# Splitting the next batch's queries inside attention, with a head's loads first on SyncE

## What is computed

```python
q = (x @ Wq.T + bq)...; k = (x @ Wk.T + bk)...; v = (x @ Wv.T + bv)...   # 16 heads of 16 dims
sim = jnp.einsum('bhid,bhjd->bhij', q, k) / sqrt(16) / (abs(temperature)[0] + 0.1)
for fi, freq in enumerate([31., 37., 41., 43., 47.]):
    scores = scores + alpha[:, fi] * jnp.sin(TWO_PI * sim / freq + phi[:, fi])
w = jax.nn.sigmoid(scores);  w = w / (jnp.sum(w, axis=-1, keepdims=True) + 1e-10)
out = jnp.einsum('bhij,bhjd->bhid', w, v)
```

## Time and profile before

| | us |
|---|---|
| median of 3 runs | 7117.2 (7109.4 to 7120.61) |
| the profiled execution's own time | 7120.0 |
| its span, first to last instruction | 7118.2 |
| projection, to attention's first DMA | 412.6 |
| TensorE, VectorE, ScalarE busy | 6113.5, 5773.2, 5853.0 |
| granted TensorE clock, mean | 0.934 |

### The profile page before, as it was taken

The page is one execution under the profiler, slowest core; times in us unless marked ns, Lnnn a source line. Parts: engine busy times, 40 slices in busy tenths (PEclk is TensorE's granted clock), DMA queues, the critical chain, the costliest instruction groups (busy, mean ns, idle before and its releaser), DMA issues. The chain is left out here.

```text
span 7118.2 us, 130314 instructions
## 1 busy us (share of the span) xinstructions
PE 6113.5 (86%) x48057; PEld 4363.9 (61%) x48057; DVE 5773.2 (81%) x4353; ACT 5853.0 (82%) x5874; POOL 205.8 (3%) x217
## 2 busy tenths in 40 slices
PE   6539999999999999999999999999999999826555
PEld 3326666666666666666666666666666666625444
DVE  6648888888888888888888888888888888857775
ACT  1139999999999999999999999999999999901111
POOL 0000000000000000000000000000000000010000
PEclk8769999999999999999999999999999999966666
DMA  7931111111111111111111111111111111131220
GB/s 291 358 143 47 47 47 46 46 47 46 45 47 45 45 47 47 47 46 47 46 47 46 47 47 46 47 45 46 47 45 46 47 45 47 30 81 46 50 52 20
DMA packets 322961, 446.10 MB, mean 63 GB/s; under 512 B 158980, under 2 KB 189604, under 8 KB 321384
## 3 DMA queue, kind: packets, MB, share of 16 engines
q1 hardware_dynamic: 317032, 432.81, 19.4%
q0 software_dynamic: 5376, 5.30, 0.3%
HBM read 284.11 MB, written 153.75 MB: 62 GB/s over the span
## 5 line engine op out<-in xcount | busy, mean ns | idle before, releaser
L593 ACT ACTIVATE a_wave<-a_ps_turn 128x1024 f32<-128x1024 f32 x5120 | 4915.0, 1365 | 132.2 <-PE a_ps_turn L527 131.9
L527 PE MATMUL a_ps_turn<-a_q_r,a_k_r 64*128 64x512 f32 x20480 | 3392.0, 399 | 399.8 <-ACT a_wave L593 249.3
L609 DVE SCALAR_TENSOR_TENSOR a_weight<-a_wave,a_head_c,a_weight 128x2048 f32<-128x2048 f32 x1536 | 3612.6, 2352 | 59.5
L527 PE MATMUL a_ps_turn<-a_q_r,a_rounder 64*128 64x512 f32 x20480 | 3241.4, 392 | 4.6 <-issue 4.6
L527 PEld LDWEIGHTS a_ps_turn<-a_q_r,a_k_r 64*128 64x128 f32 x20480 | 1951.8, 185 | 1574.9 <-ACT a_wave L593 804.5
L527 PEld LDWEIGHTS a_ps_turn<-a_q_r,a_rounder 64*128 64x128 f32 x20480 | 1976.6, 186 | 244.6 <-issue 9.4
L609 DVE SCALAR_TENSOR_TENSOR a_weight<-a_wave,a_head_c 128x2048 f32<-128x2048 f32 x512 | 1203.9, 2351 | 844.4 <-ACT a_wave L593 844.4
L587 ACT ACTIVATE a_weight<-a_weight,a_head_c 128x2048 f32<-128x2048 f32 x512 | 1186.0, 2316 | 5.2 <-DVE a_weight L609 5.2
L547 PE MATMUL a_ps_out<-a_weight,a_v_r 128*32 128x512 f32 x4096 | 547.2, 606 | 7.6 <-ACT a_weight L587 5.4
L506 POOL COPY a_head_c<-a_table 128x5 f32 (+1 forms) x128 | 114.3, 893 | 5596.2 <-ACT a_weight L587 5596.1
L547 PEld LDWEIGHTS a_ps_out<-a_weight,a_v_r 128*32 128x32 f32 x4096 | 80.8, 108 | 194.7 <-issue 184.0
(11 more groups left out here) (231 smaller groups left out, 1919.3 us busy)
## 6 DMA issues: line engine op xcount, KB each, us to landing
q_d<-p_q_hl SPq DMA_DIRECT2D x80, 1024.0 KB, 8.3
a_q_r<-q_d SPq DMA_DIRECT2D x256, 320.0 KB
a_k_r<-k_d SPq DMA_DIRECT2D x512, 128.0 KB
a_q_r<-q_d SPq DMA_DIRECT2D x256, 160.0 KB
k_d<-p_k_hl SPq DMA_DIRECT2D x8, 4096.0 KB, 15.2
a_k_r<-k_d SPq DMA_DIRECT2D x512, 64.0 KB
o_d<-a_out SPq DMA_DIRECT2D x512, 34.0 KB
num<-o_d SPq DMA_DIRECT2D x32, 512.0 KB
```

The lines of the kernel that those rows point to most:

```text
L527: last = nc.tensor.matmul(ps_turn[slot_of(r, s, f)][:, half, :], exact(w(rows[half])), exact(q_r[rows[half], k, f, :]), start=(i == 0), st ...
L593: nc.scalar.activation(wave[:, s // 2 % 2, f, s % 2, :], ps_turn[slot_of(r, s, f)][:].rearrange("p a b -> p (a b)"), ACT.Sin, scale=TURN_I ...
L609: return v.scalar_tensor_tensor(both(weight[:, i, :, :]), both(wave[:, i % 2, f, :, :]), head_c[:, k, f:f + 1], to, ALU.mult, ALU.add)
```

## The change

The projection stores the whole queries of each batch (`qk_sb` to a new `q_d` of 1 MB a batch), and splits only batch 0, whose split queries go to `qs_d`. The split of batch b+1 is made during attention over batch b: in heads 1 to 8 of the 16, two parts a head. A part is 128 features by 128 tokens (`QW`), fetched from `q_d`, scaled for all five frequencies in one TENSOR_TENSOR, rounded in a CAST, subtracted in another TENSOR_TENSOR, and stored in two DMAs. The buffers are double. The loops of SyncE and VectorE now run over batches with 16 heads written out. On SyncE the loads for the next head come first, then the stores of one part, the result's store, the stores of the second part, and the fetches of the next two parts.

```diff
@@ project_qkv, SyncE
-                def keep(b):
+                def keep(b, split=False):
+                    sp.wait_ge(q_ready, b + 1)
+                    sp.dma_start(q_d[b, :, :].rearrange("(m p) l -> p m l", p=P), qk_sb[:, 0, :, :]).then_inc(whole_kept, 16)
                     sp.wait_ge(v_ready, b + 2)
                     sp.dma_start(v_d[b, :, :, :], v_sb[:]).then_inc(v_kept, 16)
-                    for m in range(KC):
-                        for f in range(NF):
-                            sp.wait_ge(q_split, NF * (KC * b + m) + f + 1)
-                            sp.dma_start(q_d[b, :, m * P:(m + 1) * P, f, :].rearrange("i p l -> p i l"),
-                                         q_hl[:, f, :, :]).then_inc(q_kept[f], 16)
+                    if split:
+                        for m in range(KC):
+                            for f in range(NF):
+                                sp.wait_ge(q_split, NF * m + f + 1)
+                                sp.dma_start(qs_d[b, :, m * P:(m + 1) * P, f, :].rearrange("i p l -> p i l"),
+                                             q_hl[:, f, :, :]).then_inc(q_kept[f], 16)
...
@@ project_qkv, VectorE
-                with dve.Fori(0, B, 1) as b:
+                def body(b, split):
+
                     dve.wait_ge(q_summed, b + 1)
+                    dve.wait_ge(whole_kept, 16 * (b + 1))
...
-                    split_q(b, 0)
+                    if split:
+                        dve.wait_ge(q_ready, b + 1)
+                        dve.wait_ge(rate_in, 32)
+                        split_q(0)
...
-                    split_q(b, 1)
                     dve.wait_ge(k_ready, b + 2)
                     dve.wait_ge(k_kept, 16 * (b + 1))
...
+                    if split:
+                        split_q(1)
+                        dve.wait_ge(q_split, NF * KC)
+                body(0, True)
+                with dve.Fori(1, B, 1) as b:
+                    body(b, False)
@@ oscillatory_attention, SyncE
+                for m in range(KC):
+                    sp.dma_start(rate[:, m, :], tab_d[8 * m:8 * m + 8, 1, :].unsqueeze(1).broadcast_to([8, HD, NF])).then_inc(rate_in, 16)
...
+                def fetch_q(b, n):
+
+                    wait_pos(sp, q_split, H * b + n - 1)
+                    dims, cols = part_of(n)
+                    sp.dma_start(q_in[:, n % 2, :], q_d[b + 1, dims, cols]).then_inc(q_loaded[n % 2], 16)
+
+                def keep_q(b, n):
+
+                    sp.wait_ge(q_split, H * b + n + 1)
+                    dims, cols = part_of(n)
+                    for i in range(2):
+                        sp.dma_start(qs_d[b + 1, i, dims, :, cols], q_hl[:, n % 2, i, :, :]).then_inc(q_kept[n % 2], 16)
...
+                def body(b, j):
+                    ahead = not isinstance(b, int) or b < B - 1
+                    split = ahead and 1 <= j <= H // 2
+                    if ahead and j == H - 1:
+                        for k in range(2):
+                            sp.wait_ge(q_kept[k], 16 * H * (b + 1))
+                    if ahead or b == B - 1 and j < H - 1:
+                        load(b + (j + 1) // H, (j + 1) % H)
+                    if split:
+                        keep_q(b, 2 * j - 2)
+                    if not isinstance(b, int) or b or j:
+                        store(b, j)
+                    if split:
+                        keep_q(b, 2 * j - 1)
+                    if ahead and j < H // 2:
+                        fetch_q(b, 2 * j)
+                        fetch_q(b, 2 * j + 1)
@@ oscillatory_attention, VectorE
+                def split_q(b, n):
+
+                    k = n % 2
+                    dve.wait_ge(q_loaded[k], 8 * H * b + 16 * (n // 2 + 1))
+                    wait_pos(dve, q_kept[k], 16 * H * b + 32 * (n // 2))
+                    v.tensor_tensor(q_all[:], q_in[:, k, :].unsqueeze(1).broadcast_to([P, NF, QW]),
+                                    rate[:, n % KC, :].unsqueeze(2).broadcast_to([P, NF, QW]), ALU.mult).then_inc(q_step, 1)
+                    dve.wait_ge(q_step, 2 * H * b + 2 * n + 1)
+                    v.tensor_copy(q_hl[:, k, 0, :, :].bitcast(F32R), q_all[:]).then_inc(q_step, 1)
+                    dve.wait_ge(q_step, 2 * H * b + 2 * n + 2)
+                    v.tensor_tensor(q_hl[:, k, 1, :, :].bitcast(F32R), q_all[:], q_hl[:, k, 0, :, :], ALU.subtract).then_inc(q_split, 1)
...
+                        if i in (1, 3) and 1 <= j <= H // 2 and (not isinstance(b, int) or b < B - 1):
+                            split_q(b, 2 * j - 2 + i // 2)
```

More of the change, by code:

```diff
@@ L108, in project_qkv @@
         q_kept = [sem(f"q_kept{f}") for f in range(NF)]
-        k_kept, v_kept = sem("k_kept"), sem("v_kept")
+        whole_kept, k_kept, v_kept = sem("whole_kept"), sem("k_kept"), sem("v_kept")
         q_step, q_split, k_step, k_split = sem("q_step"), sem("q_split"), sem("k_step"), sem("k_split")
@@ L128, in _ @@
                     sp.sem_inc(q_kept[f], 16)
+                sp.sem_inc(whole_kept, 16)
                 sp.sem_inc(k_kept, 16)
@@ L153, in _ @@
                     sp.dma_start(rate[:, m, :], tab_d[8 * m:8 * m + 8, 1, :].unsqueeze(1).broadcast_to([8, HD, NF])).then_inc(rate_in, 16)
-                with sp.Fori(0, B // 2 - 1, 1) as pair:
+                for b in range(2):
+                    sp.wait_ge(x_turned, b + 2)
+                    load(b + 2, b)
+                    keep(b, b == 0)
+                with sp.Fori(1, B // 2 - 1, 1) as pair:
                     for k in range(2):
@@ L164, in _ @@
                 for f in range(NF):
-                    sp.wait_ge(q_kept[f], 16 * (KC * B + 1))
+                    sp.wait_ge(q_kept[f], 16 * (KC + 1))
+                sp.wait_ge(whole_kept, 16 * (B + 1))
                 sp.wait_ge(k_kept, 16 * (B + 1))
@@ L355, in _, with oscillatory_attention @@
                     last.then_inc(k_ready, 1)
-def oscillatory_attention(nc, tab_d, q_d, k_d, v_d, ph_d, o_d):
+def oscillatory_attention(nc, tab_d, q_d, qs_d, k_d, v_d, ph_d, o_d):
     U = LT
@@ L362, in oscillatory_attention @@
     HF = H * NF
+    QW = KC * L // H
     with ExitStack() as ctx:
@@ L376, in oscillatory_attention @@
         v_r = sb("a_v_r", [P, 2, LT, VP])
+        q_in = sb("a_q_in", [P, 2, QW])
+        q_all = sb("a_q_all", [P, NF, QW])
+        q_hl = sb("a_q_hl", [P, 2, 2, NF, QW])
+        rate = sb("a_rate", [P, KC, NF])
         warm = sb("a_warm", [P, 2])
@@ L412, in heads_in_turn, with heads_by_batch @@
                 body(g, g % 2, g % 3)
+        def heads_by_batch(eng, body):
+            for j in range(H):
+                body(0, j)
+            with eng.Fori(1, B - 1, 1) as b:
+                for j in range(H):
+                    body(b, j)
+            for j in range(H):
+                body(B - 1, j)
+            body(B, 0)
         LOADS = 16 * 14
@@ L453, in load @@
                     to_k = lambda row, count, i, src: sp.dma_start(k_r[row:row + count, k, i, :], src).then_inc(qk_loaded[k], 16)
-                    dims, head = bass.ds(h * HD, HD), bass.ds(h, 1)
-                    for j in range(2):
+                    dims = slice(j * HD, (j + 1) * HD)
+                    for n in range(2):
                         for i in range(2):
[L457 to L461, removed]
+                            to_k(64 * n, 2 * HD, i, k_d[b, 2 * i:2 * i + 2, dims, :])
+                            to_k(64 * n + 2 * HD, HD, i, k_d[b, 2 * i, dims, :])
+                        to_q(64 * n, 2 * HD, qs_d[b, 0:1, dims, :, halved(n)].broadcast_to([2, HD, NF, HALF]))
+                        to_q(64 * n + 2 * HD, HD, qs_d[b, 1, dims, :, halved(n)])
+                        to_q(64 * n + 3 * HD, 2, ph_d[:, j:j + 1, :, halved(n)].rearrange("i o f l -> i (o f) l"))
@@ L467, in store @@
+                def keep_q(b, n):
[3 more added lines that the diff above has]
+                        sp.dma_start(qs_d[b + 1, i, dims, :, cols], q_hl[:, n % 2, i, :, :]).then_inc(q_kept[n % 2], 16)
+                def store(b, j):
+                    g, k = H * b + j, j % 2
                     sp.wait_ge(out_ready, g)
                     for c in range(4):
-                        sp.dma_start(o_d[(g - 1) // H, c // 2, bass.ds((g - 1) % H, 1), :, halved(c % 2)].rearrange("o c l -> (o c) l"),
+                        sp.dma_start(o_d[b if j else b - 1, c // 2, (j - 1) % H, :, halved(c % 2)],
@@ L480, in _ @@
+                heads_by_batch(sp, body)
                 for k in range(2):
```

33 lines of the change are left out of this document (18 added, 15 removed).

## The result

The changed kernel takes 7018.97 us (median of 4 runs, 7016.85 to 7023.52) against 7115.22 (7109.4 to 7120.61): ratio 0.987, 95% interval 0.985 to 0.988. The sign, the range (6966 to 7024) and the forecast's mechanism in the projection and in attention hold, its size does not: 96 us were gained where 136 were forecast, and the time lies 38 us above the predicted 6981. The profiled execution spans 7018.2 us, 100.0 less than before.

| | before | after | difference | forecast |
|---|---|---|---|---|
| start to attention's first DMA | 412.60 | 270.52 | -142.1 | -137.4 |
| from there to ScalarE's first sine | 62.7 | 64.5 | +1.8 | +1.4 |
| first sine to the last copy of an output | 5747.2 | 5749.9 | +2.7 | 0 |
| that copy to the end (routed block) | 895.7 | 933.3 | **+37.6** | 0 |
| span | 7118.2 | 7018.2 | -100.0 | -136.0 |

The account below looks back on a forecast made before the run. It took the projection to be bound by split-query stores holding up VectorE, then TensorE; 7118.2 - 137.4 + 1.4 = 6982.2 of span, less 1.0 for the median, gave 6981 us, range 6966 to 7024.

Parts of the forecast that it names:

- Projection: Projection stage: without the later batches' splits and stores, TensorE's own turn of 28.26 us bounds it; gain 137.4 us.
- K's passes moved into the gap: Projection, batch 0: K's passes move ahead of the second split, where VectorE waits for stores anyway; 5.8 us saved.
- Rate loads: Between projection and attention: two loads of rates ahead of the first head's loads on SyncE; costs 1.4 us.
- Splits: Attention: 112 splits of 2.3 us, 257 us of VectorE in all, hidden in its idle time before pairs; cost 0.
- The cushion: Attention: VectorE may be 3.0 us late before ScalarE notices; 2.2 us left at each of the 112 places.
- Loads: Attention, SyncE: the next head's load starts about 1.5 us later behind new DMAs, with 12.1 us of margin; cost 0.
- the rival: Attention: stores at 53 GB/s delay the head loads, 5 us in each of 56 heads, 280 us, about 7260; chance 0.07.
- Fewer turns, longer code: Attention loops of VectorE and SyncE, now over a batch of 16 heads instead of two; cost taken as nothing.
- The routed block after attention is untouched: 0: Block after attention, whose code the change leaves alone; its time was taken to stay the same, cost 0.
- VectorE late: Attention: a split dearer than 2.76 us makes VectorE fall behind; at 3.9 us it costs 108 us, 7089; chance 0.08.
- Another bound in the projection: Projection: K's buffer, the whole-query buffer or x comes late, turns take some 34 us; 30 us less gain, 7011; chance 0.10.
- A small slow-down everywhere: Attention: the splits' stores slow everything a little; 2.4 us in each of 56 heads undoes the gain; near no change 0.03.

Follow-up runs that it names:

- mild_split: Changed kernel with one more pass of 128x640 in each of the 112 splits in attention: 6977.3 us, attention 5749.4 us.
- dear_split: Changed kernel with two more passes of 128x640 before each of the 112 splits in attention: 7080.53 us, attention 5815.2 us.
- stores_first: Changed kernel with a head's first pair of split-query stores put ahead of the next head's loads on SyncE: 7732.45 us.
- turns24: Changed kernel with TensorE's and ScalarE's attention loops written out over 24 heads with 4 turns, instead of 6 heads with 19: 6944.67 us.

## Why the prediction was right or wrong

- **Projection, right, 4.7 us too small.** The chain of stores, split, drain was the bound; with it gone, TensorE's own turn is the next one. At batch 7's start the forecast was 2.9 us late, since the turn measured 27.6 us and not the 28.26 of the first turn. From K's store to attention's first DMA it takes 12.4 us instead of 14.9; K's store has less in front of it. K's passes moved into the gap gave 6.2 us (78.56 to 72.38), forecast 5.8.
- **Rate loads, right**: issued in 1.30 us, and 1.8 more to the first sine.
- **Splits, right at 0.** 2.12 us against an estimated 2.3. The cushion was real: mild_split uses it up without loss, dear_split overruns it. The slack was sized 0.3 us a head too small, because the idle gaps with a bracket leave out the small ones.
- **Loads, right at 0.** The only wait of TensorE for a head's queries is the one at the start. What makes loads late is shown by stores_first: 714 us, by the order of the queue, not by the bandwidth that the rival put a price on. (Its sum has a slip: 768 KB at 53 GB/s take 14.8 us and not 15.7, so 4.2 us a head and 240 us, not 280.) A store lands in 4.9 us (median) after its issue; the forecast had 2.2 (by bandwidth) to 11 us for all 768 KB ahead of a load, and chose nearer to the former.
- **The terms "Fewer turns, longer code; the trace shows no wait of these two at their loop ends, so nothing for it", and "The routed block after attention is untouched: 0": wrong, and this is the whole miss.** The first looked for a price at the loops that were rewritten, and there it is indeed hidden: VectorE and SyncE have slack in attention. But the longer code pushes every later loop of that engine to another place in its program. The routed loop went from a place that costs 0.4 us a turn at its top to one that costs up to 4.5 and a second stop: 37.6 us in all. Nothing in the rows of before showed the bad case, since that kernel stood in a good place; the trace of before did show how such a stop looks, TensorE's `issue` waits at its turns (51.8 us), and I took no account of them.
- Without that term the sum would have been near: 7018.2 - 37.6 = 6980.6 of span, forecast 6982.2. In part this is luck, -4.7 in the projection against +0.4 and +2.7.
- **The rivals.** VectorE late: its condition (2.76 us a split) wasn't met. Another bound in the projection: no, from batch 2 on every turn is TensorE's. A small slow-down everywhere: attention moved by 2.7 us, within what it varies from execution to execution. None of them held the 38 us.

The Trainium skill has a rule that I didn't weigh: "Runtime: NRT & Kernel Launch", section "Instruction fetch mechanics", says that an engine holds 32 KiB of its program (512 instructions; TensorE 2048), refilled in order in blocks of 256, and that a taken branch to a target outside of it stalls until the block is fetched. With TensorE's attention loop of 2294 instructions (4503 as compiled) this agrees: about 3 us at each turn. It agrees too with the second instruction queue, `q8`, which moves packets of 16.4 KB, 422 before and after and 380 in turns24, so it does not follow VectorE's program; only TensorE's and ScalarE's programs were changed in turns24. With VectorE's routed loop of 308 (332 as compiled) it agrees in kind but not in size: packets of 8.2 KB and good places that repeat after 128 instructions point to blocks of half that size.

## What to carry to other kernels

When an edit makes one engine's program longer or shorter, compare the time of every later loop of that engine, touched or not. `issue` waits at a loop's first instruction, passes that take 4 us instead of 0.2, and packets on the instruction queue tell a loop that is fetched anew each turn; 32 idle memsets ahead of it were worth 41 us here (7018.97 against 6977.54), nearly half of what the change itself brought. Work laid into another engine's gaps is free until the sum of gaps is used up, and what decides whether its DMAs are free is what stands behind them on the issuing queue.

## What the hardware showed that was not expected

- The place of an unchanged loop of 308 VectorE instructions moved the routed block by 26 to 43 us (890.5 to 896.3 against 921.8 to 933.3), with a period of 128 instructions in all places tried. In the bad places the stop at the loop's top is 3.5 us on average in a turn (4.0 in dear_split), and a pass some 5 us later takes 4.1 to 4.5 us (in five turns of six in dear_split, in all six elsewhere); `q14` moves 5 packets a turn there and none in the good places. Three blocks of 128 kept and four fetched anew fits all kernels; a loop of another length, which would test it, wasn't tried.
- At a turn of its attention loop TensorE stood still for 2.6 to 3.3 us in after, and each turn less gave 4.7 us, by ScalarE, which was the bound. That the rest goes into filling the PSUM slots anew is a guess; no run shows it.
